# Products without a reader on TensorE at the start of two causal-attention stages

## The chip, the cores and the metric

The program runs on one core of a Trainium2 chip. The metric is the device time of one execution in microseconds (us); lower is better. The engines are TensorE (PE, with its weight loads shown apart as PEld), VectorE (DVE), ScalarE (ACT), GpSimd (POOL) and SyncE (SP, which here only issues DMAs). Each engine takes its own instructions in order and waits on semaphores for the others. TensorE's clock is granted by the chip at one of two levels, 1.2 or 2.4 GHz; the profile shows it as a share of full speed, 0.50 or 1.00.

## The reference

Eight sub-layers in a row, each of the form `x = x + f(layernorm(x))`, on 2048 rows (4 pieces of 512) of width 128. The two that matter here are causal attentions with 16 heads of 8 columns, on sequences of 512 (layer 1) and 256 (layer 2). Layer 1:

```
q = _low_rank_proj(hidden_states, q_a, q_b)
k = _low_rank_proj(hidden_states, k_a, k_b)
v = hidden_states @ v_w.T + v_b
...
att = jnp.einsum('bhtd,bhsd->bhts', q, k) * scale
att = jnp.where(causal[None, None], att, jnp.finfo(att.dtype).min)
att = jax.nn.softmax(att, axis=-1)
y = jnp.einsum('bhts,bhsd->bhtd', att, v)
...
return y @ o_w.T + o_b
```

The lines above are those of layer 1; layer 2 computes the same from weights that are themselves generated (`tanh(p) * W + B`).

## The kernel before

One program of eight stages, one after the other. Stages 2 and 4 are the causal attentions; both call `causal_attention`, so whatever is changed there is changed twice. The stage works on 16 items called quads, a quad being 4 heads of one 512-row piece. For a quad q:

- TensorE projects its queries and its keys (`project`, items `("q", q)` and `("k", q)`, line 1701): one full 128-row fp32 product of 512 columns each, into the single PSUM bank `pm` ("odd_jobs"). ScalarE takes part of the result (line 1812), VectorE writes the rest into `stacks` (line 1864), and then the bank is free for the next "odd job": `odd_bank` makes each of them wait until the one before it has been emptied.
- 12 units of scores give each row's maximum (`scores_for_max`, `("max", q, u)`, line 1720). They contract over 32 rows only. Two PSUM banks `p1` take turns: unit m waits for `s_neg`, m - 1, so until VectorE has reduced unit m - 2 (line 1884).
- The maxima are transposed (line 1729) and subtracted from the stack; then the scores are computed again, now transposed (line 1741), ScalarE takes the exponential (1821, 1824), GpSimd cuts it above the diagonal (1676), TensorE multiplies it with the values (`pv`, line 1755, into the bank `po`), turns the result (1764), and at the end of a 512-row piece projects it (1771, 1777).

The order on every engine comes from one list, `causal_plan()`. It repeats a hand-written `TEMPLATE` of 43 items and shifts each by a lag, so that in one period the last maxima of quad q + 1, the first maxima of quad q + 2, the exponentials of quad q and the product with the values of quad q - 1 stand side by side. At the start of a stage most of those don't exist yet: the first period holds only the key projection of quad 0, its first units, and the query projection of quad 1; exponentials begin in the third period and products with the values in the fourth. In front of the plan, `before_tensor` runs the preparation of the stage; in stage 2 that is 32 small products (line 1933) and 16 transposes of the normalised input (line 232), in stage 4 the transposes alone, followed by a wait for generated weights.

The loop that the change touches:

```
for item in plan:
    if item[0] in ("q", "k"):
        project(item)
    ...
    elif item[0] == "max":
        scores_for_max(*item[1:])
```

Of the kernel before, what the change touches and what calls it, by code (L numbers as in the profile page):

```python
# [19 lines left out]
P = 128  # L20
B, S, D = 4, 512, 128
# [1512 lines left out]
def max_units(u):  # L1534

    if u < 4:
        return [(u, TPC - 1, 0)]
    if u < 8:
        return [(u - 4, 0, 0), (u - 4, 2, P)]
    return [(u - 8, 1, 0)]  # L1540


def score_units(r):

    if r < 2:
        return [(2 * r + b, 0, b * S) for b in range(2)]
    if r < 4:
        return [(2 * (r - 2) + b, j, b * S + at) for j, at in ((1, 0), (3, S - P)) for b in range(2)]
    return [(2 * (r - 4) + b, 2, b * S) for b in range(2)]


def prob_place(x, j):

    if j == 2:
        return 4, x * 2 * P
    return x // 2 + 2 * (j != 0), x % 2 * S + (S - P) * (j == 3)
# [33 lines left out]
def causal_attention(sh, stage, ctx, ln, probs, p1, p2, po, pm, wst, qk_bias, s_wst, wv, wo, v_bias, o_bias, scale,  # L1590
# [9 lines left out]
    nc, tag = sh.nc, f"s{stage}"  # L1600
# [31 lines left out]
    def emptied(item):  # L1632

        what, n = item[0], item[1]
        if what in "qk":
            return s_stack, 2 * n + "qk".index(what) + 1
        return {"maxT": s_sub, "v": s_v32, "oT": s_oTs, "y": s_x}[what], n + 1

    @block.sync
    def _(sp):  # L1640
        if extra:
            sp.dma_start(extra[0], extra[1]).then_inc(extra[2], 16)
        sh.load_next(sp, stage)
# [41 lines left out]
    @block.tensor  # L1685
    def _(pe):
        pe.wait_ge(sh.wsem[stage], 16)
        before_tensor(pe)
        pe.wait_ge(ln.ready, B)
        pe.wait_ge(s_wst, 2)  # L1690

        def odd_bank(item):
            k = odd.index(item)
            if k:
                pe.wait_ge(*emptied(odd[k - 1]))

        def project(item):
            what, q = item
            c, g = divmod(q, QUADS)
            odd_bank(item)  # L1700
            nc.tensor.matmul(pm[:, :], wst["qk".index(what)][:, g * P:(g + 1) * P], sh.xnT[:, c * S:(c + 1) * S],  # L1701
                             start=True, stop=True).then_inc(s_proj, 1)

        def values(item):
            c = item[1]
            odd_bank(item)
            for i in range(TPC):
                last = nc.tensor.matmul(pm[:, i * P:(i + 1) * P], sh.xnT[:, c * S + i * P:c * S + (i + 1) * P], wv,
                                        start=True, stop=True)
            last.then_inc(s_v, 1)  # L1710

        def scores_for_max(q, u):
            m = UNITS * q + u
            if u == 0:
                pe.wait_ge(s_stack, 2 * q + 2)
            if m >= 2:
                pe.wait_ge(s_neg, m - 1)
            for x, i, at in max_units(u):
                rows, n = slice(32 * x, 32 * x + 32), (i + 1) * P
                last = nc.tensor.matmul(p1[m % 2][:, at:at + n], stacks[0][rows, q % SLOTS, i * P:n],  # L1720
                                        stacks[1][rows, q % SLOTS, 0:n], start=True, stop=True)
            last.then_inc(s_max, 1)

        def max_transposes(item):
            q = item[1]
            odd_bank(item)
            pe.wait_ge(s_neg, UNITS * (q + 1))
            for i in range(TPC):
                last = nc.tensor.transpose(pm[:, i * P:(i + 1) * P],
                                           wide[:, q % 2, i, :, :].rearrange("p x r -> p (x r)"), sh.ident[:, :])  # L1730
            last.then_inc(s_maxT, 1)

        def scores_less_max(q, r):
            n = EXPS * q + r
            if r == 0:
                pe.wait_ge(s_sub, q + 1)
            if n >= 2:
                pe.wait_ge(s_exp, n - 1)
            for x, j, at in score_units(r):
                rows = slice(32 * x, 32 * x + 32)  # L1740
                last = nc.tensor.matmul(p2[n % 2][:, at:at + S - j * P], stacks[1][rows, q % SLOTS, j * P:(j + 1) * P],  # L1741
                                        stacks[0][rows, q % SLOTS, j * P:S], start=True, stop=True)
            last.then_inc(s_sc, 1)

        def pv(q, j):
            c, g = divmod(q, QUADS)
            pe.wait_ge(s_cut, EXPS * q + {0: 2, 1: 4, 2: 6, 3: 4}[j])
            if j == 0:
                if g == 0:
                    pe.wait_ge(s_v32, c + 1)  # L1750
                if q:
                    pe.wait_ge(s_norm, q)
            for x in range(4):
                slab, at = prob_place(x, j)
                last = nc.tensor.matmul(po[32 * x:32 * x + 32, j * P:S], v32[:, c % 2, j, 4 * g + x, :],  # L1755
                                        probs[:, q % 2, slab, at:at + S - j * P], start=(j == 0),
                                        stop=(j == TPC - 1), skip_group_check=True)
            if j == TPC - 1:
                last.then_inc(s_pv, 1)

        def turn(q):
            pe.wait_ge(s_oq, q + 1)
            for i in range(TPC):
                last = nc.tensor.transpose(po[:, i * P:(i + 1) * P], oq[:, i * P:(i + 1) * P], sh.ident[:, :])
            last.then_inc(s_turn, 1)

        def turn_out(item):
            odd_bank(item)
            pe.wait_ge(s_norm, QUADS * (item[1] + 1))
            for i in range(TPC):  # L1770
                last = nc.tensor.transpose(pm[:, i * P:(i + 1) * P], o[:, i, :], sh.ident[:, :])
            last.then_inc(s_oT, 1)

        def project_out(item):
            odd_bank(item)
            for i in range(TPC):
                last = nc.tensor.matmul(pm[:, i * P:(i + 1) * P], oT[:, i * P:(i + 1) * P], wo, start=True, stop=True)
            last.then_inc(s_y, 1)

        for item in plan:  # L1780
            if item[0] in ("q", "k"):
                project(item)
            elif item[0] == "v":
                pe.wait_ge(s_ones, 2)
                values(item)
            elif item[0] == "max":
                scores_for_max(*item[1:])
            elif item[0] == "maxT":
                max_transposes(item)
            elif item[0] == "exp":  # L1790
                scores_less_max(*item[1:])
            elif item[0] == "pv":
                pv(*item[1:])
            elif item[0] == "turn":
                turn(item[1])
            elif item[0] == "oT":
                turn_out(item)
            elif item[0] == "y":
                project_out(item)
# [35 lines left out]
    def _(dve):  # L1835
# [23 lines left out]
        for item in plan:  # L1859
# [7 lines left out]
            elif item[0] == "v_done":  # L1867
                c = item[1]
                dve.wait_ge(s_v, c + 1)
                if c >= 2:  # L1870
# [4 lines left out]
                                            [P, TPC, H8, HD8]), ALU.add).then_inc(s_v32, 1)  # L1875
            elif item[0] == "max":
                _, q, u = item
                m = UNITS * q + u
                dve.wait_ge(s_max, m + 1)
# [1138 lines left out]
```

## Time and profile before

| | |
|---|---|
| time, median of 3 runs | 1861.18 us (1858.63 to 1862.11) |
| time of the profiled execution | 1858.74 us |
| its span, first to last instruction | 1855.8 us |
| mean granted TensorE clock | 0.887 |
| TensorE matmuls busy | 1515.8 us, 82% of the span |
| VectorE busy | 1171.6 us, 63% |
| ScalarE busy | 823.6 us, 44% |
| GpSimd busy | 797.0 us, 43% |

The page cuts the span into 40 slices of 46.4 us. Stage 2's plan runs from 363.6 us to some 580 us, stage 4's from 812.8 us to some 1030 us. In both, the first slices show a granted clock of about half and the following ones a full clock.

### The profile page before, as it was taken

The page shows a single profiled execution, that of the slowest core. Times are in us where ns is not written, and L with a number is a line of the kernel's source. Part 1 is how long each engine was busy: PE and PEld are TensorE (multiplying, and loading weights), DVE is VectorE, ACT ScalarE, POOL GpSimd, SP SyncE. Part 2 cuts the span into 40 slices and gives each one's busy share as a digit, 9 for nine tenths or more (in the row PEclk, how much of TensorE's full clock was granted, in tenths as well). Part 3 has the DMA queues.
Part 4 walks back from the last instruction along what each step waited for, and adds up shares of the span by engine and source line. Part 5 has one row for each costly group of instructions (what it writes and reads, how often), then busy time and mean ns, then how long its engine had stood idle before and what let it go on. Part 6 is the DMA issues. An engine that isn't in the chain of part 4 may idle for free. (4 is left out here: it accounts for less than half of the span.)

```text
span 1855.8 us, 25506 instructions
## 1 busy us (share of the span) xinstructions
PE 1515.8 (82%) x9252; PEld 927.5 (50%) x9252; DVE 1171.6 (63%) x2938; ACT 823.6 (44%) x1280; POOL 797.0 (43%) x835
## 2 busy tenths in 40 slices
PE   3676577889997999749999779979999999996194
PEld 2455455644444677514444557755554455544163
DVE  5666688568884766667886242347877868675302
ACT  3654233236663655334666333335545545441041
POOL 5441344512223755542222353325555645453633
PEclk8788699759997999856999989989999999998597
DMA  2000000100000000110000012000000000002123
GB/s 76 1 2 2 30 1 1 77 1 1 1 1 22 1 0 1 70 58 1 1 2 1 1 48 83 9 1 1 1 1 1 1 1 1 1 1 102 55 59 92
DMA packets 20828, 37.60 MB, mean 20 GB/s; under 512 B 1760, under 2 KB 18144, under 8 KB 19552
## 3 DMA queue, kind: packets, MB, share of 16 engines
q1 hardware_dynamic: 18656, 31.76, 4.9%
q0 software_dynamic: 2048, 4.21, 0.7%
q8 instruction: 74, 1.21, 0.3%
q14 instruction: 50, 0.41, 0.1%
HBM read 26.50 MB, written 9.47 MB: 19 GB/s over the span
## 5 line engine op out<-in xcount | busy, mean ns | idle before, releaser
L1884 DVE CUSTOM_DVE_ANT_0 s_masked_scores<-s_for_max,s_mask_qk 128x128 bf16<-128x128 f32 (+3 forms) x512 | 227.4, 487 | 63.4 <-PE s_for_max L1720 59.9
L2271 POOL TENSOR_TENSOR wbuf<-s_probs 128x1024 f32<-128x1024 f32 x64 | 151.9, 2373 | 207.2 <-ACT s_probs L2430 207.2
L1676 POOL TENSOR_SCALAR_AFFINE_SELECT s_probs<-s_probs 128x256 f32<-128x256 f32 x256 | 100.9, 406 | 312.4 <-ACT s_probs L1821 246.7
L2430 ACT ACTIVATE s_probs<-s_scores 128x1024 f32<-128x1024 f32 x128 | 132.2, 1033 | 202.3 <-PE s_scores L2352 202.3
L1147 POOL TENSOR_TENSOR s_hidden_lo<-s_hidden,s_hidden_hi 128x512 fp32r<-128x512 f32 x108 | 142.5, 1320 | 121.4 <-ACT s_hidden_hi L1258 121.3
L2472 DVE TENSOR_REDUCE s_negmax<-s_for_max 128x2 f32<-128x1024 f32 x126 | 152.2, 1208 | 21.3 <-PE s_for_max L2327 21.3
L1720 PE MATMUL s_for_max<-s_k_stack,s_q_stack 32*128 32x128 f32 (+3 forms) x512 | 137.9, 442 | 33.0 <-DVE s_max_wide L1884 26.7
L1720 PEld LDWEIGHTS s_for_max<-s_k_stack,s_q_stack 32*128 32x128 f32 x512 | 69.3, 205 | 169.5 <-DVE s_max_wide L1884 114.2
L2479 DVE RECIPROCAL s_recip<-s_pv_and_sums 128x128 f32<-128x128 f32 x128 | 116.6, 934 | 47.3 <-PE s_pv_and_sums L2378 47.3
L1821 ACT ACTIVATE s_probs<-s_scores 128x1024 f32<-128x1024 f32 x128 | 126.7, 1022 | 21.8 <-PE s_scores L1741 18.2
L2365 PE MATMUL s_pv_and_sums<-s_probs,s_v 128*64 128x512 f32 x512 | 123.9, 605 | 0.9 <-DVE wbuf L2487 0.9
L1274 ACT ACTIVATE s_silu<-s_gate 128x512 f32<-128x512 f32 x108 | 64.5, 597 | 120.0 <-PE s_comb L1183 110.8
L1328 DVE TENSOR_TENSOR s_gated<-s_silu,s_up 128x512 f32<-128x512 f32 x96 | 65.9, 686 | 61.1 <-ACT s_silu L1274 60.2
L1812 ACT ACTIVATE s_low_rows_hi<-s_odd_jobs,s_low_rows_bias,s_low_rows 128x512 fp32r<-128x512 f32 x64 | 49.8, 777 | 120.7 <-PE s_odd_jobs L1701 116.3
L1701 PE MATMUL s_odd_jobs<-xnT,s_w_stacked 128*128 128x512 f32 x128 | 83.8, 742 | 18.3 <-ACT s_w_stacked L2018 11.4
L1755 PE MATMUL s_pv<-s_probs,s_v_and_one 128*32 128x512 f32 (+3 forms) x1024 | 94.2, 467 | 2.2 <-DVE s_o L1903 2.2
L1741 PE MATMUL s_scores<-s_q_stack,s_k_stack 32*128 32x384 f32 (+3 forms) x512 | 84.6, 382 | 1.6 <-ACT s_probs L1824 1.5
L2276 POOL TENSOR_TENSOR xnT<-wbuf 128x1024 f32<-128x1024 f32 x32 | 78.1, 2440 | 2.5
L1258 ACT CAST s_hidden_hi<-s_hidden 128x512 fp32r<-128x512 f32 x108 | 66.2, 613 | 22.7 <-DVE s_hidden L1331 22.6
L1409 POOL TENSOR_TENSOR s_h_lo<-s_h,s_h_hi 128x512 fp32r<-128x512 f32 x32 | 42.4, 1324 | 73.7 <-DVE s_h_hi L1503 73.7
L2352 PE MATMUL s_scores<-s_q_hi,s_k_hi 64*128 64x512 f32 x256 | 64.1, 496 | 9.6 <-ACT s_probs L2430 9.6
L1331 DVE TENSOR_TENSOR s_hidden<-s_gated,s_comb 128x512 f32<-128x512 f32 x96 | 65.9, 686 | 3.3
(464 smaller groups left out, 3707.1 us busy)
## 6 DMA issues: line engine op xcount, KB each, us to landing
s_w<-extra SPq DMA_DIRECT2D x2, 2048.0 KB, 10.3
wbuf<-w SPq DMA_DIRECT2D x1, 3460.0 KB, 10.8
s_probs<-extra SPq DMA_DIRECT2D x1, 2898.0 KB, 9.6
wbuf<-w SPq DMA_DIRECT2D x1, 2888.0 KB, 15.2
wbuf<-w SPq DMA_DIRECT2D x1, 2124.0 KB, 8.1
dispatched<-s_empty_slots SPq DMA_DIRECT2D x1, 2064.0 KB, 6.7
s_rows<-dispatched SPq DMA_DIRECT2D x8, 258.0 KB, 2.8
expert_rows<-s_empty_slots SPq DMA_DIRECT2D x1, 2048.0 KB, 14.0
```

The costliest lines, as they stand in the source:

```text
L1147: nc.gpsimd.tensor_tensor(hid_lo[:, n % DEEP, :], hidden[:, n % DEEP, :], hid_hi[:, n % DEEP, :].bitcast(F32), ALU.subtract).then_inc(s_lo, 1)
L1676: last = nc.gpsimd.affine_select(out=diag, in_=diag, compare_op=ALU.is_ge, fill=0.0, base=0, pattern=[[0, diag.shape[1]], [1, P]], channel ...
L1720: last = nc.tensor.matmul(p1[m % 2][:, at:at + n], stacks[0][rows, q % SLOTS, i * P:n], stacks[1][rows, q % SLOTS, 0:n], start=True, stop= ...
L1741: last = nc.tensor.matmul(p2[n % 2][:, at:at + S - j * P], stacks[1][rows, q % SLOTS, j * P:(j + 1) * P], stacks[0][rows, q % SLOTS, j * P ...
L1755: last = nc.tensor.matmul(po[32 * x:32 * x + 32, j * P:S], v32[:, c % 2, j, 4 * g + x, :], probs[:, q % 2, slab, at:at + S - j * P], start ...
L1821: nc.scalar.activation(probs[:, q % 2, r, :], p2[n % 2][:, :], ACT.Exp, scale=scale).then_inc(s_exp, 1)
L1884: last = nc.vector.tensor_tensor_reduce(out=junk[:, m % 2, at:at + n], in0=p1[m % 2][:, at:at + n], in1=mask[:, S - n:S], scale=1.0, scala ...
L2271: nc.gpsimd.tensor_tensor(added[half], probs[:, g % 2, 2 * half, :, :], probs[:, g % 2, 2 * half + 1, :, :], ALU.add).then_inc(s_added, 1)
L2365: last = nc.tensor.matmul(po[x * dh:(x + 1) * dh, :], v[:, c % 2, j, (2 * n + x) * dh:(2 * n + x + 1) * dh], probs[:, g % 2, j, x, :], sta ...
L2430: nc.scalar.activation(probs[:, g % 2, j, :, :], p2[:, :, :], ACT.Exp, scale=dh ** -0.5).then_inc(s_exp, 1)
L2472: nc.vector.tensor_reduce(negmax[:, g % 2, :, j], max_bank(g, j)[:, :, :], AX.X, ALU.max, negate=True).then_inc(s_neg, 1)
L2479: nc.vector.reciprocal(recip[:, at], ps_sum[:, at]).then_inc(s_rec, 1)
```

## The change

A helper `keep_running(times)` issues products of 256 columns, full 128 rows by 128 columns in fp32, into the bank `po`. Nothing reads them; the first product with the values overwrites them. No engine waits for them and they wait for nothing. 14 of them stand behind the query projection of quad 0, 6 behind its key projection, and one behind each of the 12 units of quad 0. That makes 32 in a stage and 64 in the program.

```diff
@@ def causal_attention, block.tensor @@
+        def keep_running(times):
+            for _ in range(times):
+                nc.tensor.matmul(po[:, 0:S // 2], wst[0][:, 0:P], sh.xnT[:, 0:S // 2], start=True, stop=True)
+
@@ the loop over the plan @@
             if item[0] in ("q", "k"):
                 project(item)
+                keep_running({("q", 0): 14, ("k", 0): 6}.get(item, 0))
             elif item[0] == "v":
...
             elif item[0] == "max":
                 scores_for_max(*item[1:])
+                if item[1] == 0:
+                    keep_running(1)
```

TensorE in stage 2, from the transposes ahead of the plan to the key projection of quad 1, before (L1701 are projections, L1720 units of scores for maxima; a unit is one row of 512, a pair of 128 and 384, or one of 256 columns):

```order
L232 MATMUL s_for_max<-ident,s_ln_xn 128x128 x16
L1701 MATMUL s_odd_jobs<-xnT,s_w_stacked 128x512 x2
L1720 MATMUL s_for_max<-s_k_stack,s_q_stack 128x512 x4
L1720 MATMUL s_for_max<-s_k_stack,s_q_stack 128x128
L1720 MATMUL s_for_max<-s_k_stack,s_q_stack 128x384
L1720 MATMUL s_for_max<-s_k_stack,s_q_stack 128x128
L1720 MATMUL s_for_max<-s_k_stack,s_q_stack 128x384
L1701 MATMUL s_odd_jobs<-xnT,s_w_stacked 128x512
```

The same place of the changed kernel, as far as the second unit (L1706 are the added products, L1724 the units):

```order
L232 MATMUL s_for_max<-ident,s_ln_xn 128x128 x16
L1701 MATMUL s_odd_jobs<-xnT,s_w_stacked 128x512
L1706 MATMUL s_pv<-xnT,s_w_stacked 128x256 x14
L1701 MATMUL s_odd_jobs<-xnT,s_w_stacked 128x512
L1706 MATMUL s_pv<-xnT,s_w_stacked 128x256 x6
L1724 MATMUL s_for_max<-s_k_stack,s_q_stack 128x512
L1706 MATMUL s_pv<-xnT,s_w_stacked 128x256
L1724 MATMUL s_for_max<-s_k_stack,s_q_stack 128x512
```

The two projections stood next to each other in the queue; now 14 products stand between them and 6 behind them, and from then on one behind each unit. The second place is the end of the added products, where quad 1 takes over, in the changed kernel:

```order
L1701 MATMUL s_odd_jobs<-xnT,s_w_stacked 128x512
L1724 MATMUL s_for_max<-s_k_stack,s_q_stack 128x256
L1706 MATMUL s_pv<-xnT,s_w_stacked 128x256
L1724 MATMUL s_for_max<-s_k_stack,s_q_stack 128x256
L1706 MATMUL s_pv<-xnT,s_w_stacked 128x256
L1724 MATMUL s_for_max<-s_k_stack,s_q_stack 128x256
L1706 MATMUL s_pv<-xnT,s_w_stacked 128x256
L1724 MATMUL s_for_max<-s_k_stack,s_q_stack 128x512 x2
L1733 MATMUL s_odd_jobs<-ident,s_max_wide 128x128 x4
L1724 MATMUL s_for_max<-s_k_stack,s_q_stack 128x512 x2
L1724 MATMUL s_for_max<-s_k_stack,s_q_stack 128x128
L1724 MATMUL s_for_max<-s_k_stack,s_q_stack 128x384
```

After the last added product the queue is what it was: the units of quad 1, the transposes of the maxima, and everything that follows.

## Rows read from the trace of the kernel before

**Rows 1.** Page, part 2: busy tenths and clock in 40 slices.

```profile
PE   3676577889997999749999779979999999996194
PEclk8788699759997999856999989989999999998597
```

**Rows 2.** Windows: length, then PE, PEld, DVE, ACT, POOL busy, PEclk, DMA.

```profile
345.80:362.80 17.00, 16.64 (x80) 15.85 (x80) 9.52 (x58) 2.71 (x5) 9.99 (x16) 0.50 0.53 210
362.80:366.20 3.40, 1.27 (x3) 0.30 (x2) 2.44 (x3) 1.36 (x2) 3.40 (x3) 1.00 0.00 0
...
393.30:407.80 14.50, 13.46 (x48) 7.34 (x48) 9.68 (x37) 7.29 (x9) 3.47 (x9) 0.50 0.00 0
407.80:417.40 9.60, 9.49 (x41) 3.62 (x41) 4.74 (x19) 3.63 (x4) 2.04 (x6) 0.50 0.01 3
417.40:422.50 5.10, 4.56 (x38) 2.52 (x37) 4.39 (x20) 3.37 (x5) 1.21 (x3) 1.00 0.00 0
...
554.00:557.40 3.40, 2.57 (x17) 1.69 (x19) 3.35 (x19) 1.38 (x2) 0.28 (x1) 1.00 0.02 5
557.40:564.20 6.80, 6.47 (x37) 2.27 (x34) 2.10 (x8) 2.50 (x3) 2.06 (x6) 0.50 0.00 0
...
812.80:868.00 55.20, 45.89 (x140) 20.42 (x144) 33.41 (x116) 16.53 (x20) 9.38 (x18) 0.50 0.00 1
```

**Rows 3.** Timeline of PE, stage 2: start, length, instruction (a fp32 product has two records).

```profile
359.05 3.89 PE L232 MATMUL s_for_max<-ident,s_ln_xn 128*128 128x128 f32 x16
...
363.62 1.13 PE L1701 MATMUL s_odd_jobs<-xnT,s_w_stacked 128*128 128x512 f32 x2 [0.68 <-ACT xnT L245]
366.85 2.08 PE L1701 MATMUL s_odd_jobs<-xnT,s_w_stacked 128*128 128x512 f32 x2 [2.10 <-DVE s_q_stack L1864]
370.57 0.80 PE L1720 MATMUL s_for_max<-s_k_stack,s_q_stack 32*128 32x512 f32 x2 [1.65 <-DVE s_k_stack L1864]
```

**Rows 4.** Timeline of PE: key projections of quads 1 to 3, and quad 1's first unit.

```profile
379.61 1.22 PE L1701 MATMUL s_odd_jobs<-xnT,s_w_stacked 128*128 128x512 f32 x1
...
383.72 1.13 PE L1720 MATMUL s_for_max<-s_k_stack,s_q_stack 32*128 32x512 f32 x2 [0.43 <-DVE s_k_stack L1864]
...
393.28 1.22 PE L1701 MATMUL s_odd_jobs<-xnT,s_w_stacked 128*128 128x512 f32 x1
407.82 1.22 PE L1701 MATMUL s_odd_jobs<-xnT,s_w_stacked 128*128 128x512 f32 x1
```

**Rows 5.** Timeline of PE at the full clock, fourth period of stage 2.

```profile
421.65 0.38 PE L1720 MATMUL s_for_max<-s_k_stack,s_q_stack 32*128 32x256 f32 x1 [0.54 <-DVE s_max_wide L1884]
421.96 0.66 PE L1764 MATMUL s_pv<-ident,s_o_quad 128*128 128x128 f32 x4
422.46 1.02 PE L1701 MATMUL s_odd_jobs<-xnT,s_w_stacked 128*128 128x512 f32 x2
423.41 0.38 PE L1720 MATMUL s_for_max<-s_k_stack,s_q_stack 32*128 32x256 f32 x2
...
433.12 0.59 PE L1701 MATMUL s_odd_jobs<-xnT,s_w_stacked 128*128 128x512 f32 x1
```

**Rows 6.** Timeline of PE, stage 0: fp32 products of 256 columns at the full clock.

```profile
90.44 0.65 PE L598 MATMUL s_odd_jobs<-s_v,s_k_to_end 128*128 128x256 f32 x2
90.93 1.00 PE L592 MATMUL s_o<-s_v,s_pairs 128*128 128x64 f32 x8
```

**Rows 7.** Timeline of PE, start of stage 4.

```profile
812.78 2.05 PE L1701 MATMUL s_odd_jobs<-xnT,s_w_stacked 128*128 128x512 f32 x2 [11.38 <-ACT s_w_stacked L2018]
817.24 2.08 PE L1701 MATMUL s_odd_jobs<-xnT,s_w_stacked 128*128 128x512 f32 x2 [2.42 <-DVE s_q_stack L1864]
820.97 0.79 PE L1720 MATMUL s_for_max<-s_k_stack,s_q_stack 32*128 32x512 f32 x2 [1.66 <-DVE s_k_stack L1864]
```

**Rows 8.** Timeline of DVE, stage 2: the first two units reduced.

```profile
371.40 0.69 DVE L1884 CUSTOM_DVE_ANT_0 s_masked_scores<-s_for_max,s_mask_qk 128x512 bf16<-128x512 f32 x1 [0.88 <-PE s_for_max L1720]
...
372.02 0.69 DVE L1884 CUSTOM_DVE_ANT_0 s_masked_scores<-s_for_max,s_mask_qk 128x512 bf16<-128x512 f32 x1
```

## The prediction, as put on record before the run

> **What bounds the kernel now.** I read the page's slices first [rows 1]. TensorE is busy seven to nine tenths of most slices, and the clock row tells what that time is worth: in slice 9 (counted from 1: 371 to 418 us) and in slices 18 and 19 (789 to 882 us) it is five to six tenths. The windows show it sharply [rows 2]. In stage 2 the clock is at half until 362.8 us, full to 366.2, then at half until 417.4 us, then full. In stage 4 it is at half from the first projection at 812.8 to 868 us. The reader is to see that TensorE is hardly idle in that half-clock time: 13.46 of 14.50 us busy in the third period, 9.49 of 9.60 us in the part of the fourth before the rise. So half clock is not the same as an idle engine, and what filled those microseconds was mostly the scores, which use 32 of the 128 rows; the rise came when products with the values had joined.
>
> The periods, from one key projection to the next, say what the half clock costs [rows 3 to 5]. Quad 0's starts at 366.85 us, the following ones at 379.61, 393.28, 407.82 and 422.46: 12.76, 13.67, 14.54 and 14.64 us. At full clock a period with more work in it takes 433.12 - 422.46 = 10.66 us. The second to fourth periods are therefore 3.01, 3.88 and 3.98 us over that, 10.9 us together, and stage 4 shows the same shape. This is what the change could win at most behind quad 0: 21.7 us in two stages.
>
> **What the added products cost: the price of one.** The trace has no such product at this place; the nearest are those of 256 columns in stage 0, at full clock: two records start at 90.44 and the next operation starts at 90.93, 0.49 us [rows 6]. A whole product of 512 columns lets the next one start after 423.41 - 422.46 = 0.95 us [rows 5], half of which is 0.48. For products in a row with the same weights I take a little less, 0.45 us at full clock, and 0.90 at half (the projection's length goes from 1.13 to 2.08 us between the levels [rows 3]). Below nothing none can lie, since TensorE takes its instructions in order; the upper bound is that all run at half clock.
>
> **14 products behind the query projection, stage 2.** Now TensorE waits 2.10 us there, for ScalarE and VectorE to empty the odd bank [rows 3]. The query projection starts at 363.62 us, at full clock; with 0.95 + 14 x 0.45 = 7.25 us the key projection can start at 370.9 instead of 366.85: +4.0 us. The wait covers 2.3 us of the added 6.3 only. The clock should stay up over this stretch, which is full-row work without a gap, so the projection takes 1.13 and not 2.08 us: its readers are 3.1 us late.
>
> **6 products behind the key projection, stage 2.** Before, the first unit starts 370.57 - 366.85 = 3.72 us behind the key projection. Now the stack would be ready 0.95 us sooner, after 2.8 us, but the queue of TensorE needs 0.95 + 6 x 0.45 = 3.65 us. The first unit starts at 370.9 + 3.65 = 374.6, +4.0 us.
>
> **One product behind each of 12 units.** At half clock the nine units and the query projection from 370.57 to 379.61 us take 9.04 us, so without the projection's 2.0 some 0.78 us for each unit. VectorE alone could take one every 0.62 us (371.40 to 372.02 [rows 8]); TensorE's round trip with two banks is the rest. At full clock that trip would shorten, but now every unit is followed by a full-row product in the same queue. A unit of 256 columns holds the next full-row operation back by 421.96 - 421.65 = 0.31 us [rows 5]; one of 512 by about 0.1 more. With 0.45 for the added product that is 0.76 to 0.86 us. So the added products eat what the clock gives to the units: nine of them take 7.7 us, with a query projection of 0.95 it is 8.6 us against 9.04. The key projection of quad 1 starts at 383.2, +3.6 us. Behind it come three units of 256 columns with their products (2.3 us) and the projection's 0.95: quad 1's first unit stands 3.25 us behind it instead of 383.72 - 379.61 = 4.11 [rows 4]. +2.7 us.
>
> **Behind the last added product.** What is left of the second period is two full-row jobs (four transposes and a query projection) among eight 32-row units. Whether the clock stays up there is the question on which the result hangs. The row that is nearest to it is 554.00 to 557.40 us, at the end of the stage's maxima: full clock, units, scores and four transposes, TensorE busy 2.57 of 3.40 us, and from 557.4 us on half clock [rows 2]. I expect the same here: the clock falls in the second half of the second period or at the start of the third, and then it comes back only where it does now, with the products with the values. In the 9.56 us from quad 1's first unit to the third key projection full clock would save some 1.4 us (0.95 on the projection, 0.45 on the transposes, whose four cost 0.50 us at full clock [rows 5]); I take half, 0.7. So +2.0 us are left in stage 2.
>
> **Stage 4** differs in its start, which is at half clock [rows 7]. The query projection lets its follower start after about 1.85 us, at 814.6. How long the clock stays down is not shown for these products; the nearest row is stage 2's transposes, full-row work from 359.05 us that is followed by full clock at 362.8 [rows 2, 3], so 3.8 us. With the same time here, two to three products run at half clock and 11.6 at 0.45, until 822.0 us: the key projection is 4.8 us late against 817.24, the first unit (822.0 + 3.65 = 825.65 against 820.97) 4.7. From there the steps are those of stage 2, 0.7 us worse: +2.7.
>
> **The sum.** 2.0 + 2.7 = +4.7 us. The profiled execution took 1858.74 us with a span of 1855.8, so 2.9 us lie around the span and don't change; it would be 1863.4. It was 2.4 us below the median of the three runs, 1861.18; to the median the sum gives 1865.9, and I say 1866.
>
> **A rule that speaks against this.** By the row at 554 us a clock at full level is lost although TensorE works most of the time [rows 2]. The Trainium skill, in "TensorE: Matmul & The Clock Gate", section "Why this matters for your kernels", puts the loss down to idle gaps between bursts of matmuls: keep them going and the speed holds. By that rule the 64 products would do what they seem to be for. That is the first rival.
>
> **Rivals.** (1) The clock holds from quad 0 to the steady state. For it: TensorE is idle for no more than a part of a microsecond at a time in these periods. Against it: the fall at 557.4 us, and that at half clock 13.46 us of work in 14.50 did not bring it up. Price: each stage keeps its +3.6 and +4.3 us up to the second key projection and then wins up to 10.9, so 7.9 - 21.8 = -13.9 us: 1847 us. It decides at the first half-clock stretch behind quad 0's last unit: without one, this is the case. (2) The added products are hidden better than I count: TensorE overlaps them with the 32-row units until VectorE's 0.62 us is the pace. That gives back about 0.24 us on 12 units, 2.9 us a stage, 5.8 us: -1.1, 1860 us, no change. For it: weight loads run beside products. Against it: the 0.31 us of a unit before a full-row job. (3) In stage 4 the clock does not rise within the 14 products: they take 12.6 us, the key projection starts at 827.2, 5.2 us later than I count: 1871 us. For it: stage 4's plan starts behind 11.38 us of idle TensorE. Against it: nothing but full-row work stands there. (4) The later rise, with the values, shifts by a few microseconds to either side; each 3.4 us more or less at half clock is 3.4 x (1 - 10.66/14.64) = 0.9 us. This is spread, no case.
>
> **How the numbers follow.** My forecast (clock lost again behind quad 0) 0.58, rival 1 0.12, rival 2 0.20, rival 3 0.10. A difference under 0.2% (3.7 us) can't be told from none here, as the three runs alone span 3.5 us. The forecast itself, 1860 to 1870, lies for four fifths above 1864.9; with rival 3 that makes slower 0.53. Rival 1 and a little of rival 2 make faster 0.17, the rest is 0.30. The range leaves out rival 1 and a tail above: 1856 to 1871.
>
> **What would show it.** Right: in the changed trace the clock is full from stage 2's first projection through quad 0's units; key projection of quad 0 at about 371 and 822 us, quad 1's at about 383 us; a period of quad 0 no shorter than 12 us; half clock again from somewhere between 388 and 398 us until the first products with the values. Wrong: full clock through the third period, units with their product closer than 0.7 us, or half clock during the 14 products of stage 2.

## The result and the profile after

The changed kernel's median is 1867.31 us (5 runs, 1863.9 to 1870.06) against 1860.26 (5 runs) of the kernel before: ratio 1.0039, 95% interval 1.0024 to 1.0053, so 7 us slower. The forecast was 1866 us. The clock behaved as forecast, the price of one step was too low.

The page of the changed kernel, part 2, answers to [rows 1]:

```profile
PE   3676589999997999759999779879999999996194
PEclk8688699879997999967999889989999999998597
```

Slice 9 of the clock row has gone from 5 to 7, and slice 18 with 19 from 5 and 6 to 6 and 7: TensorE had more clock, and the program took longer. The mean granted clock rose from 0.887 to 0.895.

The windows at the starts of stage 2 and stage 4 of the changed kernel (columns as in [rows 2]):

```profile
362.20:365.60 3.40, 3.40 (x17) 2.98 (x17) 0.00 (x0) 0.00 (x0) 0.03 (x1) 1.00 0.00 0
365.60:389.40 23.80, 22.73 (x80) 12.69 (x79) 13.44 (x49) 2.33 (x3) 0.00 (x0) 1.00 0.00 0
389.40:416.70 27.30, 25.63 (x98) 11.80 (x98) 16.48 (x63) 13.24 (x15) 5.50 (x14) 0.50 0.00 1
416.70:422.20 5.50, 4.85 (x42) 2.53 (x39) 4.44 (x20) 3.37 (x5) 1.19 (x3) 1.00 0.00 0
819.50:846.80 27.30, 26.22 (x96) 15.81 (x95) 14.12 (x50) 2.33 (x3) 0.30 (x1) 1.00 0.00 1
846.80:874.10 27.30, 25.63 (x98) 11.66 (x99) 16.55 (x63) 13.24 (x15) 5.50 (x14) 0.50 0.00 0
```

The reader is to see 27 us of full clock from the 14 products on, in both stages, and then 27 us of half clock, until the products with the values. The fall at 389.4 us comes with TensorE busy 22.73 of the 23.80 us before it.

TensorE's timeline of stage 2 of the changed kernel, which answers to [rows 3] (L1706 are the added products, two records each):

```profile
358.35 2.07 PE L1701 MATMUL s_odd_jobs<-xnT,s_w_stacked 128*128 128x512 f32 x2 [0.68 <-ACT xnT L245]
360.21 7.15 PE L1706 MATMUL s_pv<-xnT,s_w_stacked 128*128 128x256 f32 x28
367.20 1.02 PE L1701 MATMUL s_odd_jobs<-xnT,s_w_stacked 128*128 128x512 f32 x2
368.06 2.75 PE L1706 MATMUL s_pv<-xnT,s_w_stacked 128*128 128x256 f32 x12
370.74 0.50 PE L1724 MATMUL s_for_max<-s_k_stack,s_q_stack 32*128 32x512 f32 x1
371.17 0.70 PE L1706 MATMUL s_pv<-xnT,s_w_stacked 128*128 128x256 f32 x2
371.80 0.49 PE L1724 MATMUL s_for_max<-s_k_stack,s_q_stack 32*128 32x512 f32 x1
372.22 0.70 PE L1706 MATMUL s_pv<-xnT,s_w_stacked 128*128 128x256 f32 x2
372.85 0.49 PE L1724 MATMUL s_for_max<-s_k_stack,s_q_stack 32*128 32x512 f32 x1
...
381.08 1.02 PE L1701 MATMUL s_odd_jobs<-xnT,s_w_stacked 128*128 128x512 f32 x2
...
384.84 0.53 PE L1724 MATMUL s_for_max<-s_k_stack,s_q_stack 32*128 32x512 f32 x2
```

Three prices can be read there. Products in a row: the six take 370.74 - 368.06 = 2.68 us, 0.447 each, the step to the unit behind them included. The 14 take 6.99, as the first few ran at half clock (the clock rose at 362.1). And unit with product: from 370.74 to 371.80, 1.06 us, made of 0.43 from the unit to its product and 0.63 from the product to the next unit.

The starts of the key projections give the periods. Stage 2 before (from [rows 3 to 5]) and after, stage 4 after; "q to k" is from the query to the key projection of quad 0:

| us | q to k | period 1 | 2 | 3 | 4 | 5 |
|---|---|---|---|---|---|---|
| stage 2 before | 3.23 | 12.76 | 13.67 | 14.54 | 14.64 | 10.66 |
| stage 2 after | 8.85 | 13.88 | 12.07 | 14.53 | 14.50 | 10.66 |
| stage 4 before | 4.46 | 12.77 | 13.67 | 14.54 | 14.63 | 10.66 |
| stage 4 after | 8.76 | 13.88 | 12.16 | 14.54 | 14.42 | 10.67 |

Of stage 4 of the changed kernel, the query projection and the first two key projections:

```profile
815.90 2.05 PE L1701 MATMUL s_odd_jobs<-xnT,s_w_stacked 128*128 128x512 f32 x2 [11.39 <-ACT s_w_stacked L2025]
824.66 1.02 PE L1701 MATMUL s_odd_jobs<-xnT,s_w_stacked 128*128 128x512 f32 x2
838.54 1.02 PE L1701 MATMUL s_odd_jobs<-xnT,s_w_stacked 128*128 128x512 f32 x2
```

To the fifth key projection stage 2 loses 5.6 + 1.1 - 1.6 - 0.1 = 5.0 us and stage 4 4.3 + 1.1 - 1.5 - 0.2 = 3.7 us: 8.7 together. The profiled spans differ by 6.4 (1862.2 and 1855.8), since stage 2 happened to begin 5.3 us earlier in this execution (358.35 against 363.62 us) and 3 us were lost in other places. Most of that lies at the end of stage 2: from the key projection of quad 8 to the first transposes of stage 3 the changed kernel takes 122.20 us and the kernel before 118.42, and until TensorE falls idle, 4.88 us before those transposes, the clock is at half for 17.0 us instead of 6.8 (557.4 to 564.2 us in [rows 2]):

```profile
532.80:536.20 3.40, 3.40 (x11) 1.73 (x12) 1.89 (x9) 0.56 (x2) 0.41 (x1) 0.50 0.00 0
556.70:566.90 10.20, 10.10 (x54) 4.96 (x58) 4.13 (x19) 4.58 (x5) 2.34 (x6) 0.50 0.00 0
570.30:573.70 3.40, 3.27 (x20) 0.93 (x20) 0.00 (x0) 1.54 (x3) 1.17 (x3) 0.50 0.00 0
```

The second profile of the changed kernel, below, has the same three falls. Whether the added products bring them about, so far behind the last of them, is not shown: the kernel before has one profile.

Nothing ahead of stage 2 was changed; its first projection stood anywhere from 357.3 to 366.7 us in the profiles of this study. This is why the periods, and not the spans, carry the comparison.

### The profile page after: what moved, and what is told of

The parts are those of the page before. It is cut to its first block and busy times, and to the rows that moved or that the text cites. A ratio compares the mean times of both kernels' runs of the same rounds, so it can differ in the third digit from the quotient of the medians.

```text
span 1862.2 us, 25741 instructions
## 1 busy us (share of the span) xinstructions
PE 1541.6 (83%) x9359; PEld 947.1 (51%) x9380; DVE 1169.4 (63%) x2938; ACT 824.5 (44%) x1280; POOL 798.0 (43%) x835
## 5 line engine op out<-in xcount | busy, mean ns | idle before, releaser
L1724 PE MATMUL s_for_max<-s_k_stack,s_q_stack 32*128 32x128 f32 (+3 forms) x512 | 135.1, 422 | 24.6 <-DVE s_max_wide L1891 21.9
L1724 PEld LDWEIGHTS s_for_max<-s_k_stack,s_q_stack 32*128 32x128 f32 x512 | 66.6, 196 | 158.5 <-DVE s_max_wide L1891 112.9
L1701 PE MATMUL s_odd_jobs<-xnT,s_w_stacked 128*128 128x512 f32 x128 | 78.7, 701 | 13.6 <-ACT s_w_stacked L2025 11.4
```

## The experiments

Theory A, that of the prediction: full-row products hold and raise the clock, 32-row products don't; each added product occupies TensorE; behind the last one the clock falls. Theory B: any matmul work without gaps holds the clock. Two more were set against single terms: C, that the products behind the units are free, because TensorE waits for VectorE there, and D, that holding the clock is worth nothing and products only cost. Every ratio is to the kernel before, run beside the variant on the same chip, in 5 rounds; the chip differs between the three sets of runs. Times are medians of 4 to 12 executions. The trace is of one of them, and not always a typical one: that of the first run below is its slowest (1871.59 us).

### Only the 14 and 6 products

```diff
             elif item[0] == "max":
                 scores_for_max(*item[1:])
-                if item[1] == 0:
-                    keep_running(1)
```

> Only the 14 and 6 products behind the first projections of each stage, none behind the units. Theory A (full-row products hold and raise the clock, each occupies TensorE for 0.45 us at full clock and 0.90 at half, and the clock is lost where only 32-row units stand): key projection of quad 0 at 5.6 and 4.3 us more behind the query projection than before (the changed kernel showed that), full clock until 2 to 7 us behind the first unit, then half until the products with the values; period 1 (first to second key projection) 11 to 12 us, periods 2 and 3 as before, 13.7 and 14.5. Time +9 us, 1869. Theory B (any matmul work without gaps holds the clock): full clock until the steady state, time 1850 or less.

Measured 1.0005 (0.9993 to 1.0016), 1863.46 us: no difference. Where the clock rises and falls was as theory A has it, my sum was not (1869 us). The periods were 10.33 (10.50 in stage 4), 13.68, 14.54, 14.07, behind 7.01 and 8.76 us from query to key projection. So the block costs 3.8 and 4.3 us and period 1 gives back 2.4 and 2.3; I had put down the cost without the return. Windows of this kernel:

```profile
365.70:382.80 17.10, 15.01 (x60) 10.15 (x59) 8.40 (x24) 2.97 (x5) 4.95 (x4) 1.00 0.00 1
382.80:420.30 37.50, 33.48 (x112) 15.96 (x112) 24.47 (x94) 14.08 (x17) 5.30 (x14) 0.50 0.00 1
```

The clock falls 5.5 us behind the first unit (377.26). That speaks against theory B, since TensorE has 15.0 of 17.1 us of work at full clock and then 33.5 of 37.5 at half. It doesn't settle it, as gaps of up to 0.79 us stand between the units. The next run has none.

The units without products show what VectorE's pace allows at full clock: two units start side by side, and the next two 378.54 - 377.26 = 1.28 us later, 0.64 us a unit.

```profile
377.26 0.49 PE L1724 MATMUL s_for_max<-s_k_stack,s_q_stack 32*128 32x512 f32 x2
378.54 1.11 PE L1724 MATMUL s_for_max<-s_k_stack,s_q_stack 32*128 32x512 f32 x2 [0.79 <-DVE s_max_wide L1889]
```

### The same count over 32 rows

```diff
-                nc.tensor.matmul(po[:, 0:S // 2], wst[0][:, 0:P], sh.xnT[:, 0:S // 2], start=True, stop=True)
+                nc.tensor.matmul(po[:, 0:S // 2], wst[0][0:32, 0:P], sh.xnT[0:32, 0:S // 2], start=True, stop=True)
```

on top of the run above (14 and 6, none behind units).

> As the run with 14 and 6 products alone, but they contract over 32 rows, not 128; count, columns and type are the same. Theory A: they don't hold or raise the clock. At half clock they take 0.90 us each, so the key projection stands some 11 to 14 us behind the query projection and the first unit some 7 us behind that; whole time +22 to +26 us, 1882 to 1886. Theory B (TensorE being busy is what counts): the same as with 128 rows.

Measured 1.0138 (1.012 to 1.0157), 1886.28 us. This is theory A's number (1882 to 1886), and the cleanest answer of the study. Its timeline and windows:

```profile
367.64 10.86 PE L1706 MATMUL s_pv<-xnT,s_w_stacked 32*128 32x256 f32 x28
378.43 2.08 PE L1701 MATMUL s_odd_jobs<-xnT,s_w_stacked 128*128 128x512 f32 x2
```

```profile
365.80:369.20 3.40, 2.73 (x10) 1.67 (x10) 2.44 (x3) 1.36 (x2) 3.40 (x3) 1.00 0.03 5
369.20:430.60 61.40, 56.16 (x159) 29.92 (x161) 29.90 (x112) 15.57 (x18) 6.36 (x15) 0.50 0.00 0
```

The 28 records run back to back, and the clock falls at 369.2 us in the middle of them; with 128 rows the same 28 kept it. TensorE is as busy to the profile in both cases, only the rows differ. In stage 4, which starts at half clock, the thin products didn't raise it either: it is half from the first projection at 825.84 us to 891.4 us.

### Only the products behind the units

```diff
             if item[0] in ("q", "k"):
                 project(item)
-                keep_running({("q", 0): 14, ("k", 0): 6}.get(item, 0))
```

> Only the 12 single products behind the units of quad 0, no 14 and 6. Theory A: key projection and first unit where they were before; the units start at half clock, where unit and product take 1.5 us instead of 0.79; the products raise the clock after 4 to 8 us; period 1 is 15 to 19 us, period 2 11 to 12; whole time +6 to +12 us. Theory C (the single products are free, as TensorE waits for VectorE there): period 1 12.8 us, whole time unchanged or better.

Measured 1.0101 (1.008 to 1.0121), 1882.77 us: slower than either theory had it. Period 1 was 22.37 us in both stages, period 2 16.10. The single products did not raise the clock at all:

```profile
370.26 0.79 PE L1724 MATMUL s_for_max<-s_k_stack,s_q_stack 32*128 32x512 f32 x1 [1.65 <-DVE s_k_stack L1870]
370.98 1.22 PE L1706 MATMUL s_pv<-xnT,s_w_stacked 128*128 128x256 f32 x2
372.13 0.79 PE L1724 MATMUL s_for_max<-s_k_stack,s_q_stack 32*128 32x512 f32 x1
```

```profile
365.60:427.10 61.50, 56.83 (x148) 26.65 (x152) 30.29 (x112) 15.56 (x18) 6.39 (x15) 0.50 0.00 1
```

Unit and product take 1.87 us at half clock where a unit alone took 0.79. Theory C is out for one product behind each unit: they are not free. Theory A's "raise" was too wide: such products held a full clock in the changed kernel, and here they did not bring a half one up.

### The clock held through quad 1

```diff
-                if item[1] == 0:
+                if item[1] <= 1:
                     keep_running(1)
```

> The changed kernel with the single products behind the units of quad 1 as well (24 a stage). Theory A: the clock stays full through the second period and, with some luck, the third; period 2 12 to 13 us (units with a product take 1.05 us), period 3 11.5 to 13 instead of 14.5, period 4 11 to 13 instead of 14.5; that brings back 3 to 5 us a stage of the changed kernel's loss: 1858 to 1863. Theory D (the loss of the clock behind quad 0 does not matter, the time is lost in the products alone): 8 more products a stage make it slower than the changed kernel, 1872.

Measured 1.0015 (1.0003 to 1.0027), 1865.02 us. The clock did what this was to show:

```profile
363.40:411.10 47.70, 45.97 (x183) 26.59 (x183) 28.34 (x97) 13.37 (x16) 7.66 (x12) 1.00 0.00 1
411.10:418.00 6.90, 6.71 (x26) 2.80 (x27) 3.35 (x15) 3.01 (x4) 1.58 (x4) 0.51 0.00 1
820.70:876.00 55.30, 53.21 (x249) 29.39 (x247) 34.35 (x129) 18.88 (x23) 6.32 (x16) 1.00 0.00 1
```

In stage 4 it was full from the 14 products into the steady state. Periods there: 13.87, 14.80, 11.52, 10.75. Against the changed kernel's 13.88, 12.16, 14.54, 14.42 the clock gives 3.0 and 3.7 us in periods 3 and 4, and the further products take 2.6 of it back in period 2. So rival 1 of the prediction, a held clock, does not give 1847 us when it is held with these products: with the clock full from the 14 products on, stage 4 is still level with the kernel before (104.90 us from the query projection of quad 0 to the key projection of quad 8, 105.00 before). Theory D doesn't fit either. With more products stage 4 takes 59.97 us from the query projection of quad 0 to its fifth key projection, the changed kernel 63.76; and the changed kernel's ratio in the next run (1.0037 to 1.0077) lies above this one's. The two were timed on different chips, and the changed kernel's first interval (1.0024 to 1.0053) just touches this one's, so the periods carry this reading. The time itself was above the 1858 to 1863 us that I expected.

### The changed kernel again

> The changed kernel once more, beside the smaller variants on the same chip: 1.002 to 1.005 of the kernel before; periods 13.9, 12.1, 14.5, 14.5 us in both stages, full clock until some 20 us behind the key projection of quad 0.

Measured 1.0057 (1.0037 to 1.0077), 1871.45 us, a little above what I expected. The periods were 13.88, 11.96, 14.54 and 14.60 us in stage 2 and 13.90, 12.16, 14.54, 14.42 in stage 4; the clock was full from 364.6 to 391.9 us. So the changed kernel is 7 to 11 us slower than the one before, by the two comparisons. The periods to the fifth key projection lose 5.1 and 3.7 us here, as in the first profile.

### Fewer products, placed inside waits

Three runs in which 14 and 6 became 4 and 3. The first has nothing behind units:

```diff
-                keep_running({("q", 0): 14, ("k", 0): 6}.get(item, 0))
+                keep_running({("q", 0): 4, ("k", 0): 3}.get(item, 0))
...
-                if item[1] == 0:
-                    keep_running(1)
```

> Only 4 products behind the first query projection and 3 behind the first key projection, none behind units: at full clock they end inside the waits that TensorE has there anyway (0.95 + 4 x 0.45 = 2.75 us against 3.2 to the key projection, 0.95 + 3 x 0.45 = 2.3 us against 2.8 to the stack). Theory A: in stage 2 the key projection is at most 1 us later, and full clock reaches into period 1, which takes 10.5 to 12 us; 1 to 2.5 us won there. In stage 4, which starts at half clock, seven products don't raise it, and 1 us is lost or none. Whole time -3 to 0 us, 1858 to 1861. If the products behind the projections raised the clock only by their number (14), stage 2 would look as before and the time be the same or 1 us more.

Measured 0.9987 (0.9976 to 0.9997), 1858.23 us. Period 1 was 11.00 and 11.24 us, periods 2 and 3 as before, period 4 0.7 and 0.9 us shorter. Contrary to what I wrote for stage 4, the clock did rise there, at 814.4 us, 3.5 us behind the query projection at 810.86. In period 1 seven products win 1.8 and 1.5 us where twenty won 2.4 and 2.3.

The second keeps 4 and 3 and the products behind all units of quad 0:

> The changed kernel with 4 and 3 in place of 14 and 6, the single products behind all units of quad 0 kept. The 14 and 6 cost 4.0 and 0 to 1 us beyond the waits that they fill; without that the key projection of quad 0 stands 3.3 us behind the query projection at full clock and 4.5 to 5.5 at half. Theory A: the single products keep the clock in stage 2, period 1 13 to 13.9 and period 2 12.1 as in the changed kernel; 4 to 5 us less than it in each stage: ratio 0.9985 to 1.001 to the kernel before. If stage 4's clock doesn't come up behind seven products, its period 1 is up to 20 us, and the time 1866 or more.

Measured 0.9997 (0.9983 to 1.001), 1859.01 us. Query to key projection 4.79 and 4.70 us, periods 13.01, 12.75, 14.54, 13.58. The changed kernel has 8.85 and 8.76 us there, and only the length of the blocks differs: they cost about 4 us a stage, that is nearly all of what the change had lost. Here the clock was full from 812.1 to 832.6 us. From 815.34 us on TensorE had the units with their products, the same sequence that in the run with them alone did not raise the clock.

The third puts a product behind every second unit of quads 0 and 1:

```diff
-                if item[1] == 0:
+                if item[1] <= 1 and item[2] % 2:
                     keep_running(1)
```

> 4 and 3 products behind the first projections, and one behind every second unit of quads 0 and 1, 19 a stage instead of 32. Theory A: two neighbouring units still run side by side in different row groups, so that a product costs 0.85 us for two units instead of for one; the clock is held through periods 1 to 3 as with products behind all units of both quads, at half their price. Period 1 11 us, period 2 12 to 12.5, period 3 11.5, period 4 10.7 to 13. -4 to -6 us a stage if the clock holds: 1849 to 1854. If the clock falls between them, as theory A allows where too few full-row products stand, period 2 is 14 to 15 us and the time 1860 to 1866.

Measured 0.9966 (0.9948 to 0.9984), 1853.21 us, with single runs from 1846.7 to 1864.3. In the profiled execution stage 2 was at half clock from 370.9 to 374.3 and again from 381.1 us (periods 11.55, 14.82, 15.97, 14.04), and stage 4, after a rise, from 824.8 to 845.3 (12.15, 16.46, 11.19, 10.76). So this profile shows the case in which the clock falls between the products; the median lies in the range of the other, 1849 to 1854, and the spread of the times suggests that both occur.

### Products where stage 4 waits for its weights

```diff
             ln.tensor(pe)
+            for _ in range(36):
+                nc.tensor.matmul(po[:, 0:P], sh.ident[:, :], sh.ident[:, :], start=True, stop=True)
             pe.wait_ge(s_gen, 2)
```

on top of the last one.

> As the run with every second unit, and with 36 products of 128 columns of the identity by itself ahead of stage 4's plan, where TensorE waits 11.4 us for the generated weights. Theory A: they take 8 to 12 us beside that wait, the query projection of stage 4 starts where it did and at full clock, the key projection 3 us behind it instead of 4.5 to 5.5, and period 1 of stage 4 is like that of stage 2. 2 to 3 us less than the run without them. If they run over the wait, the query projection starts later by 1 to 2 us and nothing is won.

Measured 0.995 (0.9926 to 0.9974), 1851.81 us. The start of stage 4 in this kernel:

```profile
791.44 10.68 PE L2031 MATMUL s_pv<-ident 128*128 128x128 f32 x72
802.55 1.10 PE L1701 MATMUL s_odd_jobs<-xnT,s_w_stacked 128*128 128x512 f32 x2 [0.42 <-ACT s_w_stacked L2025]
803.48 1.89 PE L1706 MATMUL s_pv<-xnT,s_w_stacked 128*128 128x256 f32 x8
807.02 1.13 PE L1701 MATMUL s_odd_jobs<-xnT,s_w_stacked 128*128 128x512 f32 x2 [1.65 <-DVE s_q_stack L1871]
```

The 36 products lie whole inside the 11.4 us wait, of which 0.42 are left, and the query projection runs in 1.10 us instead of 2.05 [rows 7]. The key projection was not 3 us behind it, as expected, but 4.47: VectorE delivers the biases of this stage late (`s_low_rows_bias`, its work from 802.85 to 805.27 us), ScalarE waits 2.90 us for them, and TensorE waits for both. Stage 4 has this wait at full clock as at half (4.46 us before), and four products fit in it.

The units of quad 0 show why a product behind every second one is cheaper than one behind each:

```profile
809.80 0.49 PE L1724 MATMUL s_for_max<-s_k_stack,s_q_stack 32*128 32x512 f32 x2 [0.36 <-DVE s_k_stack L1871]
810.22 0.70 PE L1706 MATMUL s_pv<-xnT,s_w_stacked 128*128 128x256 f32 x2
811.08 1.11 PE L1724 MATMUL s_for_max<-s_k_stack,s_q_stack 32*128 32x512 f32 x2 [0.16 <-DVE s_max_wide L1891]
```

Two units with a product take 811.08 - 809.80 = 1.28 us at full clock, the same as two units without one. So theory C holds for every second unit: such a product lies in TensorE's wait for VectorE.

What the 36 products are worth in the program's time is not shown. 2 to 3 us were expected against the run before; the medians differ by 1.4 us and the intervals overlap. In this profile stage 2's periods were 11.61, 11.51, 11.21, 10.77: 93.25 us to the key projection of quad 8 instead of 103.79. That is 10.5 us won in one stage, though the clock was at half from 373.4 to 376.8 us. Stage 4 won 6.7 us by the same measure (98.31 against 105.00), with half clock from 813.7 to 817.1 and from 841.0 to 851.2. This execution, of 1841 us, is the third fastest of twelve.

Two variants of this version close the series. With quad 2's units as well:

> The best version so far (4 and 3, products behind every second unit of quads 0 and 1, 36 products ahead of stage 4's plan) with those of quad 2 as well: 6 more a stage, in periods 2 and 3. Theory A: the clock is lost less often in periods 3 and 4, where the best version had 10 us at half clock in stage 4; the six products cost up to 0.4 us each where TensorE is the pace, 2 us a stage. Between 0.992 and 0.997; periods 11.5, 12, 11.6, 10.7. Theory D (more products only cost): 3 to 5 us more than the best version.

Measured 0.9934 (0.9908 to 0.996), 1845.86 us, the lowest of all, but spread from 1839.98 to 1867.48: in the profiled execution, its slowest, stage 2 had periods of 17.29 and 19.11 us, mostly at half clock. That its median is below that of the run before is not clear of noise. With a product behind each unit of quads 0 and 1:

> The best version with a product behind each unit of quads 0 and 1 instead of every second. The clock holds in both stages from the first projection to the steady state; period 1 13.7, period 2 14.8 (as in the run that held the clock so), period 3 11.5, period 4 10.8. Against the best version's 11.6, 11.5, 11.2, 10.8 that is 5.8 us a stage more: with the clock held in every execution some 1850 to 1856, ratio 0.995 to 0.998. It tells whether a surely held clock is worth the second product.

Measured 0.9958 (0.9942 to 0.9973), 1852.07 us, and 1849.68 to 1853.51 in all of its runs. Periods 13.12, 14.78, 11.52, 10.77, clock full from 362.3 to 550.0 us and from 802.6 to 997.2. The further products cost 5.3 us in stage 2 against the profile of the run before (98.53 and 93.26 us to the key projection of quad 8). In these five runs the time varied little; five are few to compare with the twelve of the other versions, and the run with 32 rows, which never held the clock, stayed within 5 us in four.

## Why the prediction was right

**The clock.** Full from the first products to the second half of period 2, then half until the products with the values: forecast, and read in the windows (in stage 2 it fell at 389.4 us, where 388 to 398 was said). The row on which it rested, the fall at 557.4 us behind 32-row work, was the right one to pick. That the rows make the difference was argued there and is shown by the run with 32 of them.

**Behind the query projection.** Forecast +4.0 and +4.8 us, measured +5.6 and +4.3. In stage 2 this execution's projection began at half clock (2.07 us long, not 1.13), so the step's assumption of a full clock held in one execution and not in the next; in the run with 14 and 6 alone, where it began at full clock, the step was +3.8. In stage 4 the clock rose 3.6 us behind the projection, where 3.8 was assumed from the transposes.

**One product behind each unit.** This is the mis-sized term. I took 0.76 to 0.86 us for unit and product and so a period of 12.3 us; measured were 1.06 us for a unit of 512 columns and a period of 13.88. The way from the unit to its product was right (0.43 us against "0.31 and 0.1 more"); the way back was not. I used the price of a product among its like, 0.45; between two 32-row units it is 0.63. Some 0.2 us for each of nine units makes up the 1.6 us by which the period was off, in each stage.

**Behind the last product.** Forecast 1.6 us won in period 2, from 3.6 late to 2.0 late; measured 1.6 and 1.5. The size is in part luck. From the second key projection to quad 1's first unit I had counted on 0.86 us and 0.35 were won (384.84 - 381.08 = 3.76 us against 4.11), as three units with their product stand there and each has the same 0.2 us too little. From that unit to the third key projection I took half of what a full clock could give, 0.7 us, and 1.26 were won, with the clock full for 4.6 of its 8.3 us. The two errors cancel. Period 3 is unchanged, as forecast; period 4 is 0.1 and 0.2 us shorter.

**The sum.** +4.7 us forecast; +8.7 in the periods of the profile, +7.05 in the medians. The extra 4.0 us is the unit term, 3.2, and the half clock at stage 2's start, 1.6, less 0.5 in stage 4's block and 0.3 in period 4. So 1866 us is closer to the measured 1867.31 than the terms are to theirs: periods and program lost 1.5 to 1.9 times what was forecast, and the median before, of five runs instead of three, came out 0.9 us lower. The second measurement, 1871.45 us, stands just above the stated range of 1856 to 1871.

**The rivals.** Rival 1 (clock held) did not occur, and its price was wrong as well: I had subtracted the whole difference between half and full clock and had not added products in quad 1, without which the clock was not held here. Rival 2 (products hidden) is out with the 1.06 us. Rival 3 (no rise within the 14) is out with the rise at 819.5 us. Among the chances one sum is off: four fifths of 0.58 and 0.10 for rival 3 make 0.56 for slower, not 0.53. The Trainium skill, in "TensorE: Matmul & The Clock Gate", section "Why this matters for your kernels", names idle gaps between bursts as what loses the speed. The traces here don't agree that this is all: the 28 records of 32 rows had no gap and lost it.

What stays open: why single products between units held a full clock in one run and left a half one where it was in another. It isn't so in every profile: in the one with the 36 products stage 2's clock was at half from 373.4 us and came back at 376.8, behind one product and a query projection (373.80 and 374.81), while in the run with single products alone a product and a query projection (380.56 and 381.57) brought nothing. No run was made that would tell why.

## What to carry to other kernels

Filling TensorE to keep its clock pays only inside waits that are there anyway: price each added product against the wait that it fills, and stop where the wait ends (4 and 3 products won two thirds or more of what 14 and 6 won in period 1, and with the products behind the units they cost 4 us a stage less). Use all 128 rows, and put the filler behind a group of narrow products, not behind each one (1.28 us for two units with a product between the pairs, twice 1.06 with one behind each). Look for a long wait just ahead of a stage that starts at half clock, and compare such kernels by periods and in many runs, since the clock's moment of falling differs between executions.

## What the runs showed of the hardware that was not expected

- Work on 32 of 128 rows did not hold the clock: 28 such records back to back over 10.86 us lost it after 1.6 us; 28 records of 128 rows kept it.
- The same sequence of units and single products held a full clock over a whole period (812.1 to 832.6 us) and left a half clock at half for a whole period (22.37 us).
- An fp32 product of 256 columns takes 0.43 us among its like (14 in 373.72 - 367.68 = 6.04 us, in the run with 14 and 6 alone) and 0.63 between two 32-row products. Behind each unit it makes 1.06 us of the 0.64 that a unit needs; behind every second one it adds nothing.
- A version that in its profile loses and regains the clock spread widely: 1840 to 1867 us in twelve runs, against 1854 to 1865 in 23 of the kernel before beside it. That the moments at which the clock falls make the spread is likely from the profiles, not shown.
